# A start-up that builds looked-up weights: where a table of powers comes from, how squares are summed over partitions, and when the weights are loaded

## The reference

```python
x  = L0_attn_x                            # (8, 1024, 512) float32
xn = layernorm(x)
# attention without softmax over positions, 3 heads, one decay each
q = xn @ Wq;  gate = softmax(xn @ Wg)
for i in range(3):
    k = xn @ Wk[i];  v = xn @ Wv[i];  decay = sigmoid(decay_logits[i])
    w = decay ** max(t - s - 1, 0) where s and t stand in the right order, else 0
    blended += gate[..., i] * ((q @ k.T) * w) @ v
s = blended @ Wo * out_scale
# ffn whose three weight matrices are lookups: weight = lut[idx], 16 values, 1376 hidden units
g = silu( (silu(xn @ lut[gate_idx].T) * (xn @ lut[up_idx].T)) @ lut[down_idx].T )
out = x + s * g
```

## Time and profile before

| | |
|---|---|
| median of 3 runs | 1879.73 us |
| profiled execution | 1879.49 us, span 1877.5 us |
| outside the span | 2.0 us |
| PE busy | 1833.9 us, 98% |
| DVE, ACT, GpSimd busy | 1221.7, 653.5, 647.8 us |
| mean granted TensorE clock | 0.993 of 2.4 GHz |
| chain that ended last | PE 93%, DMA 2%, DVE 1% |

### The profile page before, as it was taken

The page is one execution under the profiler, slowest core; times in us unless marked ns, Lnnn a source line. Parts: engine busy times, 40 slices in busy tenths (PEclk is TensorE's granted clock), DMA queues, the critical chain, the costliest instruction groups (busy, mean ns, idle before and its releaser), DMA issues.

```text
span 1877.5 us, 39471 instructions
## 1 busy us (share of the span) xinstructions
PE 1833.9 (98%) x14216; PEld 1252.0 (67%) x14216; DVE 1221.7 (65%) x2565; ACT 653.5 (35%) x1176; POOL 647.8 (35%) x641
## 2 busy tenths in 40 slices
PE   5799999999999999999999999999999999999999
PEld 1237758485776858586685858677594867768485
DVE  7686748485774848476584848668484856748374
ACT  2584334142433424242342414243342424334131
POOL 9212506143340705234160613326060432506021
PEclk9899999999999999999999999999999999999999
DMA  9975736465663736565472646547373655647250
GB/s 230 231 280 138 180 95 188 100 161 128 158 164 104 194 85 167 136 158 148 118 198 79 174 124 156 145 130 187 88 184 103 162 136 148 170 99 200 65 141 26
DMA packets 349254, 275.98 MB, mean 147 GB/s; under 512 B 216496, under 2 KB 253744, under 8 KB 348992
## 3 DMA queue, kind: packets, MB, share of 16 engines
q1 hardware_dynamic: 337664, 266.57, 53.9%
q0 software_dynamic: 11408, 6.89, 2.6%
HBM read 204.16 MB, written 30.93 MB: 125 GB/s over the span
## 4 chain that ended last, share of the span: by engine, by line
PE 93%; DMA 2%; DVE 1%; SPq 1%; POOL 1%; ACT 1%; issue 0%; POOLq 0%; DVEq 0%; ACTq 0%
PE F L1568 43%; PE F L1597 24%; PE B L1456 15%; PE B L1488 2%; PE B L1461 2%; PE B L1462 2%; PE B L1463 2%; DMA blocks<-ring 1%; PE F L1379 1%; POOL codes L617 1%; PE F L1461 1%; PE F L1462 1%; PE F L1463 1%; DMA xt<-codes 0%; DVE region L1006 0%
## 5 line engine op out<-in xcount | busy, mean ns | idle before, releaser
L1568 PE MATMUL F<-xtc,ring 128*128 128x256 f16 (+1 forms) x4224 | 497.7, 273 | 0.0
L1568 PEld LDWEIGHTS F<-xtc,ring 128*128 128x128 f16 (+1 forms) x4224 | 416.1, 100 | 42.4
L1597 PE MATMUL F<-wd_hi,region 128*128 128x512 f16 (+1 forms) x1408 | 429.2, 379 | 0.0
L1568 PE MATMUL F<-xt,ring 128*128 128x256 f16 (+1 forms) x3168 | 377.5, 273 | 0.0
L1568 PEld LDWEIGHTS F<-xt,ring 128*128 128x128 f16 (+1 forms) x3168 | 310.0, 100 | 34.4
L1597 PE MATMUL F<-wd_lo,region 128*128 128x512 f16 (+1 forms) x704 | 266.7, 379 | 0.0
L1597 PEld LDWEIGHTS F<-wd_hi,region 128*128 128x128 f16 (+1 forms) x1408 | 137.6, 98 | 162.6
L1354 DVE SCALAR_TENSOR_TENSOR region<-F,row_out,region 128x512 f32<-128x512 f32 x64 | 48.0, 750 | 291.2 <-ACT region L933 291.2
L684 POOL TENSOR_TENSOR rstd<-var,nhalf 128x4 f32<-128x4 f32 x15 | 15.4, 1026 | 625.8 <-DVE var L964 625.8
L690 POOL TENSOR_TENSOR region<-region 128x512 f16<-128x512 f32 x96 | 122.3, 1273 | 221.9 <-ACT region L765 221.9
L933 ACT ACTIVATE region<-F,scale_hf 128x512 f32<-128x512 f32 x64 | 44.0, 688 | 435.5 <-PE F L1597 435.5
(11 more groups left out here) (203 smaller groups left out, 2958.7 us busy)
## 6 DMA issues: line engine op xcount, KB each, us to landing
ring<-blocks SPq DMA_DIRECT2D x546, 256.0 KB, 3.1
x_sb<-in_x SPq DMA_DIRECT2D x64, 256.0 KB, 3.4
out_y<-x_sb SPq DMA_DIRECT2D x64, 256.0 KB, 2.0
ring<-blocks SPq DMA_DIRECT2D x112, 128.0 KB, 2.5
blocks<-ring SPq DMA_DIRECT2D x35, 256.0 KB, 7.5
x_sb<-codes SPq DMA_DIRECT2D x10, 512.0 KB, 8.4
chalf<-codes SPq DMA_DIRECT2D x9, 512.0 KB, 8.8
xt<-codes SPq DMA_DIRECT2D x9, 512.0 KB, 8.8
```

Of the source, the lines that this page charges most:

```text
L1568: ins = T_.matmul(out_, a, b, start=fresh, stop=False, skip_group_check=True)
L1597: ins = T_.matmul(bf[:, :], a, b, start=(k == 0 and n == 0), stop=(k == FC - 1 and n == 2))
```

## The change

- `fade`: PE makes the row of powers of each head on all 128 partitions (three matmuls whose stationary operand is one column of `fade_s` broadcast), ACT copies 128x384 values into `faded`, and GpSimd writes two halves to DRAM from all partitions: zeros from `state`, powers from `faded`. The table in DRAM is laid out `[128, 3, 256]`. `state` is zeroed in DVE's unit 8 instead of after the loop.
- `squares`: GpSimd's sum over partitions goes. A tile of ones (in `mixed`, after the fade is turned) and one matmul on PE, the last piece of unit 22, sum the squares; ACT copies five columns.
- Scales are made by DVE at unit 26 instead of 25, ACT's high parts at units 25 to 29 instead of 26 to 30.
- The weights' loads go with SP's units 12 to 15 instead of 16 to 19.
- The wait for the last stored sum moves from ahead of the groups to ahead of the second product (the first k) in a group.

```diff
+    PIECES.setdefault(22, []).append(("squares", 0, 0))
...
-        if s in (None, "x", "fade"):
+        if s in (None, "x", "fade", "squares"):
             return 3
...
-        fade_row, fade_end = mask[0:NH, 1], mask[0:NH, 2]
-        fade_both = mask[0:NH, 1:3].rearrange("p a t -> p (a t)")
-        fade_rows = nc.dram_tensor("fade_rows", [NH, P, 2 * P], F32, kind="Internal")
+        fade_row = faded[:, :].rearrange("p (h t) -> p h t", h=NH)
+        ones = mixed
+        fade_rows = nc.dram_tensor("fade_rows", [P, NH, 2 * P], F32, kind="Internal")
...
-        HIGH_AT = {26: 0, 27: 1, 28: 2, 29: 3, 30: WO}
+        HIGH_AT = {25: 0, 26: 1, 27: 2, 28: 3, 29: WO}
-        SCALES_AT = 25
+        SCALES_AT = 26
-        WEIGHTS_AT = {16: 0, 17: 1, 18: 2, 19: 3}
+        WEIGHTS_AT = {12: 0, 13: 1, 14: 2, 15: 3}
...
             pool.wait_ge(s_sum, NTH["fade", 0, 0] + 1)
-            pool.dma_start(fade_rows[:, :, :], fade_both.unsqueeze(1).broadcast_to([NH, P, 2 * P])).then_inc(s_row, 16)
-            pool.wait_ge(s_sq, 5)
-            G_.partition_all_reduce(gsum[:, :], amax[:, 0:5], P, RADD).then_inc(s_gsum, 1)
+            G_.memset(ones[:, :], 1.0).then_inc(s_const, 1)
+            pool.wait_ge(s_st, 1)
+            pool.dma_start(fade_rows[:, :, P:2 * P], state[:, :].rearrange("p (h t) -> p h t", h=NH)).then_inc(s_row, 16)
+            pool.dma_start(fade_rows[:, :, 0:P], fade_row).then_inc(s_row, 16)
             pool.wait_ge(s_pick, 2 * CG)
-            pool.wait_ge(s_row, 16)
-            pool.dma_start(mask[:, :, :], bass.AP(fade_rows, P, [[2 * P - 1, P], [2 * P * P, NH], [1, P]])).then_inc(s_mask, 16)
+            pool.wait_ge(s_row, 32)
+            pool.dma_start(mask[:, :, :],
+                           bass.AP(fade_rows, P, [[2 * P * NH - 1, P], [2 * P, NH], [1, P]])).then_inc(s_mask, 16)
...
-                    copy(fade_row, bank[0:NH, 0:P], scale=2.0 ** SP).then_inc(s_sum, 1)
+                    copy(faded[:, :], bank[:, 0:HD], scale=2.0 ** SP).then_inc(s_sum, 1)
+                elif s == "squares":
+                    copy(gsum[:, :], bank[:, 0:5]).then_inc(s_sum, 1)
...
                 if b == NORM_AT:
                     norm(0, 16 * GT, 0)
+                    V_.memset(state[:, :], 0.0).then_inc(s_st, 1)
...
                 if b == SCALES_AT:
-                    dve.wait_ge(s_gsum, 1)
+                    dve.wait_ge(s_sum, NTH["squares", 0, 0] + 1)
...
-            V_.memset(state[:, :], 0.0).then_inc(s_st, 1)
...
-                T_.matmul(B[3][0:NH, 0:P], fade_s[:, :], flip[:, :], start=True, stop=True,
+                for h in range(NH):
+                    ins = T_.matmul(B[3][:, h * P:(h + 1) * P], fade_s[:, h:h + 1].broadcast_to([P, P]), flip[:, :],
+                                    start=True, stop=True, skip_group_check=True)
+                ins.then_inc(s_psum, 1)
+
+            def add_squares():
+                if BUSY["squares", 0, 0]:
+                    pe.wait_ge(s_sum, BUSY["squares", 0, 0])
+                pe.wait_ge(s_const, 4)
+                pe.wait_ge(s_sq, 5)
+                T_.matmul(B[3][:, 0:5], ones[:, :], amax[:, 0:5], start=True, stop=True,
                           skip_group_check=True).then_inc(s_psum, 1)
...
                     elif j == 0:
                         pe.wait_ge(s_st, gi * GT + 1)
+                    else:
+                        pe.wait_ge(s_sum, len(ORDERED))
...
-            pe.wait_ge(s_sum, len(ORDERED))
```

More of the change, by code:

```diff
@@ L11 @@
 I32 = mybir.dt.int32
-RADD = bass.bass_isa.ReduceOp.add
 P = 128
@@ L324, in attention_ffn_kernel @@
         s_sq = sem("squares_ready")
-        s_gsum = sem("norms_ready")
         s_lscale = sem("lut_scales_ready")
@@ L630, in _ @@
             G_.memset(flip[:, :], 0.0).then_inc(s_cstep, 1)
-            G_.memset(fade_end, 0.0).then_inc(s_cstep, 1)
-            pool.wait_ge(s_cstep, 6)
+            pool.wait_ge(s_cstep, 5)
             G_.affine_select(out=eye4, in_=eye4, compare_op=ALU.not_equal, fill=1.0, base=0,
@@ L659, in _ @@
             pool.wait_ge(s_dec, 3)
-            pool.wait_ge(s_cstep, 9)
+            pool.wait_ge(s_cstep, 8)
             for m in (fade_s, fade_t, fade_tile):
@@ L1443, in _ @@
                         turn_fade()
+                    elif s == "squares":
+                        add_squares()
                     elif s == "x":
```

## The result

| | time, us | ratio to before (95%) |
|---|---|---|
| before | 1879.64, median of 6 (1877.73 to 1880.05) | |
| changed | 1871.85, median of 6 (1870.91 to 1873.47) | 0.9962 (0.9950 to 0.9973) |
| forecast | 1866.0 | 0.9927 |

A forecast was written before the change was run, and what follows sets the result against it. PE, busy 98%, bounds the groups, so only the first 141 us could be won, where a blocked DRAM write held ACT. 12.2 + 2.3 - 1.9 + 0.6 - 0.5 + 1.0 = 13.7 us saved gave 1866.0 us, range 1862.5 to 1869.5.

The forecast's parts named there:

- The hole and its cause: Start-up, 74 to 86 us: ACT waits on a block write held up by the three-partition table write; removing it gains 12.2 us.
- Behind the hole: Units 18 to 22: ACT's idle time for the last wv and another write goes, gaining 2.3 us (0 to 3.5).
- The squares' wait: End of unit 22: the squares' matmul waits until ACT has stored the transposed x, costing 1.9 us (1.5 to 2.4).
- The weights' loads: SP's units 12 to 15: nine issues move ahead, codes still arrive nearly in time; -0.5 us (-3 to 0).
- The bound that I had worked out: Weights' loads term if casts and codes pay for the loads, as transfers share the same 16 engines: up to -6.6 us.
- High parts one unit earlier: ACT's first copy moves into unit 25; ACT, the bound from 118 us, has one less: +0.6 us (0 to 0.7).
- The last wait: Start of the groups: the first product starts sooner after PE's last piece, gaining 1.0 us (0.3 to 1.3).
- The rest: Table's two writes 6 us each; fade matmuls, later scales and earlier zeroing cost nothing; groups as long as before.
- The signs: Expected: no 74 to 86 us gap, block writes within 11 us, unit 22 stored near 91, first product near 128 us.
- Slower: Rival, 4%: weights' loads block SP's queue ahead of the codes between 38 and 56 us; 1880 to 1886 us, say 1883.
- The hole closes only in part: Rival, 17%: DMAs become the bound after the hole, 5 to 8 us return as waits; 1871 to 1875, say 1872.

The follow-up runs named there:

- e3: The kernel before with only the rows of powers made on all partitions, the table written from there and the state zeroed early: 1867.19 us, ratio 0.9945.
- e7: e5 plus an unread 384 KB GpSimd write from three partitions in the old shape, right behind the table's two writes: 1878.71 us, ratio 1.0003.
- e1: The changed kernel with the weights' loads back at SP's units 16 to 19: 1869.26 us, ratio 0.9952.
- e6: The changed kernel with SP issuing a unit's block writes ahead of its weights' loads: 1870.95 us, ratio 0.9955.
- e4: The changed kernel with the squares' matmul in the bank of the S3 sums, so it need not wait for the stored x: 1868.22 us, ratio 0.9944.
- e5: The changed kernel with the edits of e1 and e4 together: 1865.32 us, ratio 0.9929.
- e2: The kernel before with only the weights' loads moved to SP's units 12 to 15: 1875.19 us, ratio 0.9984.
- e9: e5 with ACT's high parts back at units 26 to 30: 1863.92 us, ratio 0.9926.

## Why the prediction was right and wrong

**The hole and its cause: right.** The prediction gave 12.2 us for the write of the three rows; the marks show 12.2 between units 16 and 17. e3 takes that one transfer away and wins 10.9 us, e7 adds one of its shape and loses 13.4. That this transfer from three partitions does it, and not its bytes or its moment, is shown. Which feature of its shape does it isn't (e7), nor that the copy lies on three DMA engines: no trace names the engines. The Trainium skill (DMA: Bandwidth & Descriptors, section "Why a DMA increments its semaphore by 16 and not by 1") would have it so, and the shares agree: 0.36 to 0.55 of the engines busy in the stretches shown beside landings of 18 to 20 us (0.47 over 74 to 86 us), against 1.0 with 401 GB/s without it (e3).

**Behind the hole: right.** 2.3 forecast, 2.7 measured, ACT at work without a gap from unit 17 to unit 22.

**The squares' wait: right, and more than the sum said.** -1.9 forecast, -2.0 in the changed trace: PE's gap is 1.62 us and ACT's store follows. That the clock fell behind so short a gap in two other traces (e1, e6), for another 1.3 us, was not in the sum.

**The weights' loads: the step that failed.** The prediction had -0.5 us, with -3 as the far end. The trace has -5.3 at unit 16. I followed the codes through SP's queue and left out the block writes behind them. For the codes the step was right: DVE waited 1.7 us for those of unit 13 and began its compare of unit 14 at 60.31, against 60.35 before. The first set's first write went from 42.23 to 53.20 us. In the trace before it was wanted at 60.5; with 9 us to land that left 9 us of room. The seven issues ahead of it had taken 8.95 us in the trace before; less SP's gap of 2.8 ahead of the codes of unit 14, it would have gone near 48.4 and landed near 57.4. That is a cover of 3 us, as thin as the one that I did count, and I should have named it. It was worse: a late cast cost 3.4 us, the issue of codes 14 alone took 3.78 us where I had taken 0.5, and the write landed after 11.2 us. In the hole the clock went to 0.50 for some 10 us, and unit 13's delay of 4.0 had grown to 5.3 by unit 16.

The bound that I had worked out beside the Trainium skill's rule (same page, section "Issuing engines are not separate DMA queues"), up to -6.6, was nearer than my term. How much of the delay is that sharing of engines and how much the order in SP's queue, the traces don't tell: of the 14.7 us by which the write was late 7.6 arose in SP's queue and 3.7 in landing, but issues get longer there too (3.78 us), and e6, with only the order changed, wins nothing by unit 16. Over the whole kernel the move costs 2.9 us between the medians of e4 and e5 and 2.6 between those of the changed kernel and e1. In the traces of e4 and e5 it is 7.8 us at unit 16 and 6.1 at unit 22: part is made up behind the hole, and e4's trace is its slowest run. With the old table it's a gain of 2.9 (e2).

**High parts one unit earlier: wrong in sign.** +0.6 forecast, -0.85 measured. I took ACT for the bound from 118 us on, as it had no idle time there. It was PE: in the kernels without the move PE has no gap in those units, and in those with it two, 0.76 us together (e5 has the move, e9 not, and the step is 29.85 against 29.01). An engine without idle time needn't be the bound when the one beside it has none either.

**The last wait: right** in the trace, +1.0 forecast, +0.95 measured; the clock was at 0.50 for the first matmuls in both.

**The rest** went as said: the two writes in 6 to 7 us, nothing for three fade matmuls, nothing for DVE's later scales, groups as long as before. The two kernels with repairs stand at 13.0 (e5) and 13.1 us (e9), next to the forecast's 13.7, but that is luck: they no longer pay the 1.9 us of the squares and the 0.5 of the loads, so the forecast's own terms make 16.1 for them. In e5's trace behind the hole only 1.0 us came instead of 2.3, and the high parts cost 0.85 us.

**The signs.** The prediction had said what would show it wrong, and most of it came: a hole of several us with the table's writes short, "the cause was another"; a block's write of over 11 us; unit 22 stored at 95.73 instead of near 91, and the first product at 133.89 instead of near 128.

**The rivals.** "Slower" named the right mechanism, SP's queue blocked by loads, with the wrong victim (codes instead of block writes) and too high a price. "The hole closes only in part" has the time, 1872, but not its cause: behind the old hole's place ACT had no gap, and the time was lost in a second hole ahead of it.

## What to carry to other kernels

When a DMA is moved up an in-order queue, go through everything behind it on that queue, to the next wait that someone has on any of it, writes and not only the loads that look urgent. One transfer of 384 KB from three partitions held up others for 12 us here (before, e7): make the data on 128 partitions, if an engine has the time. Before something is moved off an engine that is late but hidden, ask who waits for it; the sum over partitions made DVE wait 0.35 us in e3 and nobody else, and its replacement put PE behind ACT.

## What the runs showed of the hardware

A gap of PE of 1.62 us was followed by the lower clock in two of the three traces that have it: e1 (0.50 from about 96.2 to 99.4 us, 32 lookups in 3.1 us instead of 1.8) and e6, not in the changed kernel. In e7 PE was idle for over 4 us before the clock fell. So a gap of that length went both ways here, and what decides it isn't shown. SP's issue of one DMA took from 0.4 us to 4.07 (codes, at 52.11 in e6); what makes an issue long isn't shown either. Two executions of the same order of instructions can differ by 3.9 us in when the codes of unit 12 are issued (37.29 in e4, 41.15 in the changed kernel), and in the latter it was a cast landing late that held them.
